# Loading the first operands of a vision tower in two halves, with four constant products ahead of them

## The reference, cut to what matters

```python
h = patchify(x) @ W.T + b                       # 1152 x 768 times 768 x 192: the embedding
h = h + attention0(layernorm(h))                # q, k, v of width 192; scores within an image
h = h + moe0(layernorm(h))                      # shared expert + 2 of 8 routed, width 768
h = h + attention1(layernorm(h))                # 12 heads, cumulative sums over the sequence
h = h + moe1(layernorm(h))                      # shared expert + 2 of 3 routed, width 384
```

## Time and profile before

| | |
|---|---|
| median of three runs | 566.83 us |
| lowest and highest of them | 561.97, 567.05 us |
| span of the profiled execution | 564.3 us |
| TensorE busy | 518.0 us (92%) |
| VectorE busy | 376.2 us (67%) |
| ScalarE busy | 256.7 us (45%) |
| GpSimd busy | 230.4 us (41%) |
| transfers, mean over the span | 115 GB/s |

### The profile page before, as it was taken

One profiled execution on the slowest core, in us unless ns is written; L12 is line 12 of the kernel. 1 busy time (PEld: TensorE's weight loads), 2 busy tenths in 40 slices (PEclk: granted clock), 3 DMA queues, 4 the chain that ended last, 5 costly groups with the idle time before them and its releaser, 6 DMA issues.

```text
span 564.3 us, 9739 instructions
## 1 busy us (share of the span) xinstructions
PE 518.0 (92%) x3430; PEld 493.6 (87%) x3430; DVE 376.2 (67%) x892; ACT 256.7 (45%) x531; POOL 230.4 (41%) x194
## 2 busy tenths in 40 slices
PE   5799896989999999999999979998996889999996
PEld 5798895989999999999999869786775789999995
DVE  1665848756666666656664587699977765566665
ACT  0337463315544555445543234984750463254331
POOL 1403100746566577656766313486743100041200
PEclk9999959899999999999999989999798799899998
DMA  8750000847465676557662503000201000000001
GB/s 337 259 227 1 2 0 1 314 126 258 144 235 199 225 257 249 196 201 255 216 253 76 189 3 153 2 2 1 77 1 51 28 0 2 2 0 2 1 21 43
DMA packets 22634, 65.03 MB, mean 115 GB/s; under 512 B 6432, under 2 KB 15008, under 8 KB 19776
## 3 DMA queue, kind: packets, MB, share of 16 engines
q1 hardware_dynamic: 20192, 59.55, 29.9%
q0 software_dynamic: 2400, 4.93, 2.5%
HBM read 55.50 MB, written 8.97 MB: 114 GB/s over the span
## 4 chain that ended last, share of the span: by engine, by line
PE 56%; DVE 10%; DMA 4%; POOL 4%; issue 3%; ACT 2%; SPq 0%; DVEq 0%; POOLq 0%; ACTq 0%
PE psum L665 17%; PE psum L448 10%; PE psum L685 10%; PE psum L1074 4%; PE psum L465 4%; PE psum L1106 3%; PE psum L1089 2%; PE psum L472 2%; DMA slots_out<-YO,XR 2%; PE psum L1131 2%; DMA XR<-marked_rows 1%; POOL w0l L728 1%; PE psum L701 1%; POOL w0t L726 1%; DVE OW L2009 1%
## 5 line engine op out<-in xcount | busy, mean ns | idle before, releaser
L728 POOL TENSOR_TENSOR w0l<-stage,w0h 128x768 fp32r<-128x768 f32 x34 | 62.5, 1839 | 81.9 <-ACT w0h L712 69.6
L685 PE MATMUL psum<-w0d,a0h 128*128 128x192 f32 x492 | 84.7, 331 | 1.3 <-DVE a0h L767 1.3
L685 PEld LDWEIGHTS psum<-w0d,a0h 128*128 128x128 f32 x492 | 81.2, 193 | 1.6 <-DVE a0h L767 1.6
L760 DVE TENSOR_SCALAR a0t<-psum 128x256 f32<-128x256 f32 (+1 forms) x114 | 50.8, 445 | 42.6 <-PE psum L665 42.4
L739 ACT ACTIVATE psum<-psum 128x256 f32<-128x256 f32 x96 | 35.3, 368 | 85.3 <-PE psum L665 81.3
L665 PE MATMUL psum<-XWh,w0h 128*128 128x256 f32 x192 | 56.1, 292 | 0.0
L665 PE MATMUL psum<-XWh,w0t 128*128 128x256 f32 x192 | 54.4, 283 | 0.0
L665 PE MATMUL psum<-XWl,w0h 128*128 128x256 f32 x192 | 53.9, 281 | 0.0
L665 PE MATMUL psum<-XWl,w0t 128*128 128x256 f32 x192 | 53.9, 281 | 0.0
L665 PE MATMUL psum<-XWh,w0l 128*128 128x256 f32 x192 | 53.8, 280 | 0.0
L448 PE MATMUL psum<-X,w1h 128*128 128x384 f32 x144 | 50.1, 348 | 1.5 <-DVE a1hf L603 1.5
(11 more groups left out here) (261 smaller groups left out, 1290.8 us busy)
## 6 DMA issues: line engine op xcount, KB each, us to landing
stage<-moe0w SPq DMA_DIRECT2D x18, 1536.0 KB, 7.2
w0d<-moe0d SPq DMA_DIRECT2D x18, 576.0 KB, 3.9
stage<-moe1w SPq DMA_DIRECT2D x4, 1056.0 KB, 4.9
marked_rows<-zero SPq DMA_DIRECT2D x4, 772.0 KB, 13.1
patch<-patches SPq DMA_DIRECT2D x4, 768.0 KB, 8.1
XR<-marked_rows SPq DMA_DIRECT2D x16, 192.0 KB, 3.5
G<-slots_out SPq DMA_DIRECT2D x6, 288.0 KB, 4.4
XR<-marked_rows SPq DMA_DIRECT2D x16, 65.0 KB, 3.7
```

The source lines that it names most:

```text
L685: last = nc.tensor.matmul(dst, A0["h"][qpar][:, fc, t * P:(t + 1) * P], W0[par]["down"][:, fc, :], start=(fc == these[0]), stop=(fc == the ...
L728: ins = engine.tensor_tensor(W0[par]["l"][:, mat, :], src, W0[par]["h"][:, mat, :].bitcast(F32), ALU.subtract)
L760: nc.vector.tensor_scalar(A0["t"][fc % 2][:, 0:width], bank[2 + fc % 2][:, 0:width], LIMIT, -LIMIT, ALU.min, ALU.max).then_inc(S0["clip_re ...
```

## The change

The embedding weights are loaded in two transfers, contraction steps 0 to 2 and steps 3 to 5, and patch block 0 in two transfers likewise; the order is weights' first half, patches' first half, weights' second half, patches' second half. Each half has a semaphore of its own. The other transfers follow in their old order. TensorE waits for the first halves ahead of step 0 of tile 0, and for the second halves ahead of its step 3; the other tiles of block 0 wait for nothing more.

VectorE, as its first instruction, fills `Y[:, 0, :]` (128 x 256) with ones. TensorE waits for that and runs four products of this tile with itself, 256 columns each, into PSUM bank 7, whose result nobody reads. VectorE waits for them ahead of `normal(0, 0)`, which writes Y anew.

```diff
+WARM = 4
@@
-        ld_tokw, ld_const, ld_row, ld_wo = sem("ld_tokw"), sem("ld_const"), sem("ld_row"), sem("ld_wo")
+        ld_tokw, ld_head = ([sem(f"{name}{i}") for i in range(2)] for name in ("ld_tokw", "ld_head"))
+        ld_const, ld_row, ld_wo = sem("ld_const"), sem("ld_row"), sem("ld_wo")
+        filled, warmed = sem("filled"), sem("warmed")
@@
-            sp.dma_start(tokw_sb[:], tokw).then_inc(ld_tokw, 16)
+            for i in range(2):
+                ks = slice(i * PATCH_K // 2, (i + 1) * PATCH_K // 2)
+                cols = slice(i * P * PATCH_K, (i + 1) * P * PATCH_K)
+                sp.dma_start(tokw_sb[:, ks, :], tokw[:, ks, :]).then_inc(ld_tokw[i], 16)
+                sp.dma_start(patch[:, cols], patches[:, cols]).then_inc(ld_head[i], 16)
             for j, (t0, t1) in enumerate(PBLK):
                 a, b = t0 * P * PATCH_K, t1 * P * PATCH_K
-                sp.dma_start(patch[:, a:b], patches[:, a:b]).then_inc(ld_patch[j], 16)
-                if j == 0:
+                if j:
+                    sp.dma_start(patch[:, a:b], patches[:, a:b]).then_inc(ld_patch[j], 16)
+                else:
                     sp.dma_start(row[:], rows).then_inc(ld_row, 16)
                     sp.dma_start(const[:], consts).then_inc(ld_const, 16)
@@
-                if tiles[0] == t0:
+                if j and tiles[0] == t0:
                     pe.wait_ge(ld_patch[j], 16)
@@
                     for k in range(PATCH_K):
+                        if j == 0 and t == 0 and k % (PATCH_K // 2) == 0:
+                            pe.wait_ge(ld_tokw[2 * k // PATCH_K], 16)
+                            pe.wait_ge(ld_head[2 * k // PATCH_K], 16)
@@
-            pe.wait_ge(ld_tokw, 16)
+            pe.wait_ge(filled, 1)
+            for _ in range(WARM):
+                last = nc.tensor.matmul(bank[7][:, 0:256], Y[:, 0, 0:P], Y[:, 0, :], start=True, stop=True)
+            last.then_inc(warmed, 1)
@@
+            nc.vector.memset(Y[:, 0, :], 1.0).then_inc(filled, 1)
             dve.wait_ge(ld_const, 16)
@@
             embedded(2)
+            dve.wait_ge(warmed, 1)
             normal(0, 0)
```

## The result

The changed kernel took 572.77 us in the median of four runs (569.59 to 575.21), the kernel before 564.46 (561.97 to 567.05). The ratio is 1.0146, with a 95% interval of 1.0098 to 1.0194: slower by 8.3 us, where 1.5 us less was forecast. It lies outside the range. The profiled execution spans 573.4 us against 564.3, so it shows a loss of 9.1 us.

What follows compares the result with a forecast made beforehand. TensorE's two opening idle stretches were taken as the bound, the second waiting for VectorE's Y. Halving 0, fill and products 0, earlier pause end -1.5 us: 566.83 - 1.5 = 565.3 us, range 560.0 to 568.5.

Steps and rivals of the forecast that it cites:

- The first halves: Opening loads: first halves of weights and patches land at 5.0 us, second halves at 6.7 as before.
- The cost of two more transfers: Load queue: everything behind is issued 0.9 us later, but nothing waits for an issue; taken as 0, otherwise 0.9.
- Fill and products: Kernel start: TensorE starts at about 1.1 us, four products take 3.4 us, hidden in the wait; cost 0.
- the fast case of block 0: TensorE's opening: at the full clock, block 0's other 18 products take 2.9 us, to 9.7; otherwise about 11.4.
- VectorE's chain: Before the transposes: statistics escape GpSimd's wait, root at 18.9 us, Y's copy ends at 24.4; gain 1.5 us.
- the step that chose 24.4 over 22.9: Last copy into Y: GpSimd holds it up, ending at 24.4 us; gain 1.5 instead of 3.0.
- The clock: TensorE after its second pause: one low-clock stretch as before, costing 1.7 us at most; taken as no change.
- The step that failed: From 26.02 us on: work depends on other work alone, so an earlier start arrives at the scatter and the end.
- The sum: Whole kernel: halving 0, fill and products 0, pause ended earlier -1.5 us; expected median 565.3 us.
- The rivals: Whole kernel: more passes (563.8 us, chance 0.17), nothing passes (566.8, 0.23), slower (570.2, 0.10).
- slower: Opening loads: halved rows move slower and delay the queue, +3.4 us, a loss beyond 1.5 us longer; chance 0.10.
- The chance of 0.03 for slower by over 1%: Measured median: slower by over about 5.7 us, from slow transfers with a high draw; chance 0.03.

Runs made afterwards that it cites:

- e_split: The changed kernel without the fill, the four products and their waits, only the halved loads: 567.92 us, ratio 1.0103.
- e_again: The changed kernel run once more, unaltered, on chip A: 570.9 us, ratio 1.0167 to the kernel before.
- h_again: The changed kernel run again, unaltered, on chip C: 569.28 us, ratio 1.0105 to the kernel before.
- i_again: The changed kernel run a third time, unaltered, with more rounds, on chip A: 570.82 us, ratio 1.0106.
- f_before_half: The kernel before with nine of the scatter's 18 transfers left out (each token's second pick), so it computes less: 560.4 us, ratio 0.9908.
- g_one16: The changed kernel with sixteen one-column products instead of four of 256 columns, on chip B: 561.76 us, ratio 0.9969.
- e_late: The kernel before with four products of 192 columns added in TensorE's second pause, no fill, chip A: 569.67 us, no ratio.
- h_one4_late: The changed kernel with its four products one column wide, plus four of 192 columns in TensorE's second pause, chip C: 569.62 us, ratio 1.0094.
- i_one4_late: The changed kernel with its four products one column wide, plus four of 192 columns in the second pause, chip A: 570.14 us, ratio 1.0111.
- e_warm: The kernel before with only the fill and the four products added, loads not halved, chip A: 571.79 us, ratio 1.0172.
- f_before: The kernel before, unchanged, run and traced a second time on chip A: 564.51 us, ratio 0.9991.
- f_after_half: The changed kernel with nine of the scatter's 18 transfers left out (each token's second pick), so it computes less: 558.74 us, ratio 0.9901.
- g_one4: The changed kernel with its four products one column wide instead of 256, on chip B: 562.45 us, ratio 0.9978.

## Why the prediction was wrong

**The first halves** were to land at 5.0 and the second at 6.7. TensorE could start at 5.32 and 7.58. The cost of two more transfers was taken as 0, with 0.9 as the other end ("if it passed on in full it would be 0.9"). It passed on almost in full: block 1 began at 10.92 instead of 10.1, and `wa` was taken up at 17.02 instead of 16.28. The term was mis-sized by 0.7 to 0.9 us. Whether the later issues did it ("Nothing waits for an issue") or slower transfers isn't shown: the last half, issued at 2.12 us against the 1.19 of the whole block before, was itself already 0.8 us late.

**Fill and products** were right: 1.18 against 1.1, 3.78 us long against 3.4, and hidden. They also brought the fast case of block 0: its last 18 records took 3.16 us (2.9 forecast), and TensorE was through tile 6 at 20.94 instead of 22.31, where e_split, without them, ended at 22.36.

**VectorE's chain** was right in its mechanisms. VectorE in the changed kernel, 17 to 26 us, and GpSimd beside it, which answer to the earlier trace rows:

```profile
17.30 0.17 DVE L1617 TENSOR_SCALAR ve<-mv 128x4 f32<-128x4 f32 x1
...
19.92 0.18 DVE L1622 RECIPROCAL rstd<-sd 128x4 f32<-128x4 f32 x1 [0.34 <-ACT sd L1195]
20.14 3.19 DVE L1624 TENSOR_SCALAR Y<-H,mv,rstd 128x192 f32<-128x192 f32 x4
23.36 1.83 DVE L1627 COPY Y<-Y 128x256 f32<-128x256 f32 x1
```

```profile
20.94 1.98 POOL L1474 TENSOR_TENSOR L1w<-stage,L1w 128x792 fp32r<-128x792 f32 x1
23.06 1.97 POOL L1477 TENSOR_TENSOR L1w<-stage,L1w 64x792 fp32r<-64x792 f32 x1
```

The statistics got free of GpSimd (0.17 us instead of 1.42). The reciprocal wasn't held up (0.18 us inside an operation). The copy was: 1.83 us instead of 0.29, ending 0.16 us after GpSimd's at 25.03, as the step that chose 24.4 over 22.9 said. This also agrees with the rule of the Trainium skill that was named there (page "SBUF — State Buffer", section "Who interferes with whom"). The root came at 19.61, not 18.9: the table load waited for the splits of `wa`, which was 0.74 late. That is the transfers' error passed on, and with it the transposes came at 25.33, not 24.5. Of the 1.5 us, 0.7 was left. TensorE's 1.4 us at tile 6 bought nothing more, since VectorE's Y ends the pause.

**The clock** was taken as no change. In this trace the transposes were in the low clock as well (granted 0.50): 1.94 us instead of 1.06, and the stretch from 27.20 to 30.60 stood at 0.54 (0.50 before). That took the last 0.7, and project_qk was at 32.44 instead of 30.9. It varies: e_again, h_again and i_again took 6.3 us from the transposes to project_qk, just the 6.35 of the forecast, and i_again had it at 31.40. The length of the pause alone doesn't decide it: f_before_half has the slow transposes behind 2.73 us, g_one16 no low clock at all behind 3.19. e_late, h_one4_late and i_one4_late show what the step was worth, 1.7 us in the 24 records, with products in the pause; g_one16 had the same 4.07 us without them.

**The step that failed** is the first one: "That work depends on other work alone, on no clock time: what starts earlier at 26.02 should arrive earlier at the scatter near 97 us and at the end." The row of TensorE from 60 to 97.3 doesn't cover the stretch behind it, where TensorE runs beside the scatter and can be held without a wait for other work that the profile shows. There 72 records took 22.7 us instead of 11.86; TensorE was 10.9 us late behind them, and 8.7 us of it remained. The sum had no term for this. What the experiments show is that on chip A the fill and the products are enough for it without the halved loads (e_warm, 571.79 us), and that four products in the second pause made three of four executions as slow (e_late). How so little work brings a longer stall stays open. The prediction read no view of 97 to 125 us, and the one of before would not have shown the stall.

A smaller slip: the forecast set the span of 564.3 us beside the measured times, but a time is about 1.8 us above the span of the same execution (575.21 and 573.4 after). The profiled one was thus near the median, not 2.5 us under it. The sum doesn't depend on it.

How much of the spread between executions is the stall isn't shown. With half the scatter left out, ten executions spread by 3.5 us for the kernel before (f_before_half) and by 5.7 for the changed one, where ten of the full kernel have 10 (f_before). But nine of those ten spread by 6.3 only, and on chip B, where none of four traces has a stall, 19 executions of the kernel before spread by 7.4 us.

**The rivals** had the right sign once, in "slower", by a mechanism that didn't take place: the halved transfers cost 0.8 us, not 3.4, and e_warm without them is as slow as the changed kernel. The threshold that rival named, 1.5 us, wasn't reached. The chance of 0.03 for slower by over 1% came from adding up known terms. It had no room for a term that the trace of before didn't hold.

## What to carry to other kernels

One trace shows one way that an execution can go: a second trace of the same kernel before had a stall that the first had not. Before a gain of 1 to 2 us is forecast from one profile, take a second one, and repeat the comparison on more than one chip: one kernel took 562.45 us on one and 571.65 on another. Look at what runs beside a long row of GpSimd's indirect transfers; that moving TensorE's longest unbroken work away from it would help is a guess that no run tried. An idle wait of TensorE can be filled with products that end inside it, but what the fill gains in the clock counts only where TensorE is what the next stage waits for. At the start of the kernel it made block 0 faster, and VectorE's Y took the gain back; in e_warm, with 1.65 us of idling behind the fill, the 84 records took 15.46 us, as before.

A median that moves by the forecast amount doesn't prove the forecast: f_after_half beat f_before_half by 1.7 us in the median, and in the traces it was 1.5 us behind at the down projections.

## What was not expected of the hardware

**TensorE can be held beside GpSimd's indirect transfers.** While the 18 transfers are issued, 1.27 us apart, TensorE's starts fall to 0.7 us apart or multiples of it, no semaphore is waited for, and other engines take up its results up to 10.2 us late. The first of these comes before the first gap: ScalarE takes up products ending at 106.57 only at 108.67. The break came 15 to 18.5 us behind the scatter's first issue in 13 traces, on chips A and C and in the first comparison, and not at all in the four traces on chip B, in the two with half the scatter, and in one of the kernel before. What is held inside TensorE isn't shown. One candidate is the fetching of instructions. The Trainium skill, page "Runtime: NRT & Kernel Launch", section "Instruction fetch mechanics", says that they come in blocks of 16 KiB and that this is mostly hidden. The trace has such blocks as transfers of their own (queue q8, 25 in the changed kernel's run, 0.41 MB): the fifth came at 113.6 us in the kernel before and at 124.1 in the changed one. A late block is rather what the stall brings than its cause. In all ten stalled traces with products at the start the fifth block came 3.6 to 12 us behind the break, when 34 to about 38 of the 72 records had run, and in f_after_half and g_one4, which have no stall, when 31 had run: it goes with TensorE's place in its stream. But in the other three (e_split, e_late, f_before) it came 1.1 to 2.1 us ahead of the break, in f_before after about 46 records, where the first trace of before had it after 33. So for these a late block isn't excluded. Another candidate is the path of signals and records: the Trainium skill, page "NOTIFIC — the notification-queue block", section "The write path", says that its internal pipeline holds an engine back rather than lose a record. No run here shows that. Which of the two it is, if either, and why it goes by the chip, stays open. So does which part of the scatter matters, GpSimd's issuing or the rows that are moved.

**A second place that goes either way** lies at 420 to 450 us. Matched instruction by instruction with the first trace of before, the changed kernel's first trace loses another 1.4 us between 421 and 432, and h_again wins 1.9 between 440 and 446 (us of the trace of before). h_again is 5 us behind by then, so the same work is in its stretch from 445 to 455. The two stretches (busy time and records of each engine, granted clock, transfer share, GB/s), the kernel before first and then h_again:

```profile
440.00:450.00 10.00, 8.96 (x33) 8.61 (x32) 6.39 (x20) 3.75 (x8) 2.20 (x2) 0.66 0.01 2
```

```profile
445.00:455.00 10.00, 7.05 (x40) 6.42 (x40) 8.19 (x23) 4.39 (x9) 2.33 (x2) 1.00 0.01 2
```

The clock stands at 0.66 over the one and at 1.00 over the other. The changed kernel's first trace has the same low stretch 9 us later (449 to 459, 0.66). Whether it falls there goes with 1.9 us here, more than the whole gain that was forecast.

**One-column products of fp32 are slow**: 0.22 us for each record (13.82 us for 64), against 0.47 for 256 columns at the same place. The time isn't in the columns alone.
